# Graph-network kernel: the one-hot compares of the edge counting in four pieces of 8 slots instead of one of 32

## The reference, cut to what matters

```python
edge_index = jnp.stack([src, dst])
x = _layernorm(x + L0(x, src, dst, ...))          # attention over incoming edges
x = _layernorm(x + L1(x, edge_index, 3))          # three times: mean of the neighbours
x = _layernorm(x + L2(x, edge_index, edge_attr))  # edge network, maximum over edges
x = _layernorm(x + L3(x, edge_index))             # three times: normalised sum of the neighbours

# of L1 and L3, three times each:
summed = jax.ops.segment_sum(x[src], dst, num_segments=N)

# L0, the attention:
aij = (feat[dst] - feat[src]) @ (w2_W.T @ a_vec) + ...
m = jax.ops.segment_max(aij, dst); aexp = jnp.exp(aij - m[dst])
alpha = aexp / segment_sum(aexp, dst)[dst]
res = segment_sum(alpha[:, None] * (feat[src] @ w2_W.T + w2_b), dst)
```

## Time and profile before

| | us |
|---|---|
| median of 3 runs | 15430.6 (15423.8 to 15435.31) |
| span of the profiled execution | 14066.3 |
| of which POOL gathers in this stage, first start to last start | 495.7 to 5414.8 |
| POOL busy over the whole span | 8729.6 (62%) |
| PE busy | 9466.4 (67%) |
| DVE busy | 8214.5 (58%) |
| ACT busy | 6584.2 (47%) |

### The profile page before, as it was taken

The page is one execution under the profiler, slowest core; times in us unless marked ns, Lnnn a source line. Parts: engine busy times, 40 slices in busy tenths (PEclk is TensorE's granted clock), DMA queues, the critical chain, the costliest instruction groups (busy, mean ns, idle before and its releaser), DMA issues. The chain is left out here.

```text
span 14066.3 us, 164878 instructions
## 1 busy us (share of the span) xinstructions
PE 9466.4 (67%) x47732; PEld 6096.5 (43%) x47732; DVE 8214.5 (58%) x5617; ACT 6584.2 (47%) x6430; POOL 8729.6 (62%) x7438
## 2 busy tenths in 40 slices
PE   2355555555555552999998477767767674999998
PEld 2244444444444442555554233333333332555555
DVE  2366666666666666787877233333333333778877
ACT  1244444444444443888886122222222221888887
POOL 5777777777777776232324777777777776142323
PEclk7555555555555555999999666666666665999999
DMA  5233333333333332999998233333333332999998
GB/s 88 48 89 86 89 86 89 86 89 86 89 87 88 87 88 70 311 296 312 294 312 243 49 65 65 65 65 65 65 65 65 65 64 44 312 301 305 295 312 259
DMA packets 3238421, 1981.98 MB, mean 141 GB/s; under 512 B 1212287, under 2 KB 3140913, under 8 KB 3238257
## 3 DMA queue, kind: packets, MB, share of 16 engines
q1 hardware_dynamic: 2785457, 1664.63, 41.5%
q0 software_dynamic: 239424, 185.44, 7.5%
q10 hardware_dynamic: 213504, 131.51, 3.3%
HBM read 1602.28 MB, written 381.54 MB: 141 GB/s over the span
## 5 line engine op out<-in xcount | busy, mean ns | idle before, releaser
L624 POOL DMA_INDIRECT attend_and_count_rows<-table,attend_and_count_ring x3136 | 3917.4, 1249 | 1029.6 <-issue 1002.7
L1230 POOL DMA_INDIRECT judge_edges_rows<-table,judge_edges_ring x3128 | 2951.6, 944 | 1013.5 <-issue 988.6
L1133 POOL DMA_INDIRECT base<-slot_sums,last_slot x588 | 1273.2, 2165 | 2914.7 <-DMA slot_sums<-propagate_mean_out 1364.4
L659 PE MATMUL attend_and_count_counts<-attend_and_count_hot_hi,attend_and_count_hot_lo 128*128 128x98 bf16 x15680 | 1377.0, 264 | 2377.5 <-ACT attend_and_count_stage L769 1501.9
L1340 DVE TENSOR_TENSOR_SCAN judge_edges_feat<-judge_edges_keep,judge_edges_feat,judge_edges_p_feat 32x512 f32<-32x512 bf16 x782 | 960.1, 1265 | 2495.6 <-PE judge_edges_p_feat L1284 2474.3
L659 PEld LDWEIGHTS attend_and_count_counts<-attend_and_count_hot_hi,attend_and_count_hot_lo 128*128 128x128 bf16 x15680 | 1154.9, 130 | 2598.6 <-ACT attend_and_count_stage L769 1626.6
L1039 PE MATMUL propagate_mean_p_dense<-propagate_mean_part,propagate_mean_split 128*96 128x512 bf16 x9114 | 1994.3, 380 | 199.3 <-ACT propagate_mean_part L966 174.8
L1039 PE MATMUL propagate_norm_p_dense<-propagate_norm_part,propagate_norm_split 128*96 128x512 bf16 x9114 | 1992.8, 380 | 188.7 <-ACT propagate_norm_part L966 158.6
L966 ACT CAST propagate_norm_part<-propagate_norm_raw 128x7168 bf16<-128x7168 uint8 x282 | 1720.0, 6162 | 337.8 <-DVE propagate_norm_slot_sum L1088 296.1
L966 ACT CAST propagate_mean_part<-propagate_mean_raw 128x7168 bf16<-128x7168 uint8 x282 | 1720.0, 6162 | 336.7 <-DVE propagate_mean_slot_sum L1088 295.3
L687 DVE TENSOR_TENSOR attend_and_count_hot_hi<-ramp_hi,attend_and_count_key_hi 128x3136 bf16<-128x3136 bf16 x490 | 878.0, 1792 | 1359.8 <-ACT attend_and_count_key_lo L737 1349.0
(11 more groups left out here) (236 smaller groups left out, 10196.0 us busy)
## 6 DMA issues: line engine op xcount, KB each, us to landing
propagate_mean_raw<-matrix SPq DMA_DIRECT2D x651, 896.0 KB, 6.5
propagate_norm_raw<-matrix SPq DMA_DIRECT2D x651, 896.0 KB, 6.5
matrix<-attend_and_count_stage SPq DMA_DIRECT2D x245, 784.0 KB, 3.9
scan<-attend_and_count_out SPq DMA_DIRECT2D x784, 68.0 KB
inject<-attend_and_count_zeros SPq DMA_DIRECT2D x196, 256.0 KB, 2.0
attend_and_count_rows<-table,attend_and_count_ring POOLq DMA_INDIRECT x3136
judge_edges_rows<-table,judge_edges_ring POOLq DMA_INDIRECT x3128
judge_edges_rows<-inject SPq DMA_DIRECT2D x782, 64.0 KB
```

What stands on the lines that cost most here:

```text
L624: nc.gpsimd.indirect_dma_start(out=rows[:, u, g, j, :], out_offset=None, in_=D.table0[:, :], in_offset=rows_of(ring[:, u, g, j:j + 1])).th ...
L659: last = nc.tensor.matmul(counts[:, r % 2, k // 4, NH * (k % 4):NH * (k % 4) + NH], hot_lo[:, u, slot, :], hot_hi[:, u, slot, :], start=Tr ...
L1133: nc.gpsimd.indirect_dma_start(out=sums[:, h, :], out_offset=None, in_=D.slot_sums[0:blocks * BLOCK, :], in_offset=rows_of(S.last_slot[:, ...
L1230: nc.gpsimd.indirect_dma_start(out=rows[:, u, half, j, 0:FEAT], out_offset=None, in_=D.table2[:, :], in_offset=rows_of(ring[:, u, half, j: ...
```

## The change

Each sub's two compares become eight: for each quarter of 8 slots first `hot_hi`, then `hot_lo`, each with its own increment of `hot`, which now goes up by 8 for each sub. PE waits for a quarter's two compares before that quarter's matmuls. ACT's wait is rescaled to the new count. Elements compared, values, matmuls and casts are the same.

```diff
             def count(i, m):
...
-                pe.wait_ge(hot, s * 2 + 2)
                 for r in range(QUARTERS):
+                    pe.wait_ge(hot, s * (2 * QUARTERS) + 2 * (r + 1))
                     pe.wait_ge(staged[r % 2], s * 2 + r // 2)
...
                 dve.wait_ge(counted[u], n * QUARTERS)
-                for hots, ramp, two, width in ((hot_hi, S.ramp_hi, key2_hi, NH), (hot_lo, S.ramp_lo, key2_lo, P)):
-                    nc.vector.tensor_tensor(
-                        hots[:, u].rearrange("p v (h t) -> p v h t", t=2),
-                        ramp[:].rearrange("p (h t) -> p h t", t=2).unsqueeze(1).to_broadcast([P, SUB, width // 2, 2]),
-                        two[:, u].unsqueeze(2).to_broadcast([P, SUB, width // 2, 2]), ALU.is_equal).then_inc(hot, 1)
+                for r in range(QUARTERS):
+                    some = slice(r * SLOTS_Q, (r + 1) * SLOTS_Q)
+                    for hots, ramp, two, width in ((hot_hi, S.ramp_hi, key2_hi, NH), (hot_lo, S.ramp_lo, key2_lo, P)):
+                        nc.vector.tensor_tensor(
+                            hots[:, u, some].rearrange("p v (h t) -> p v h t", t=2),
+                            ramp[:].rearrange("p (h t) -> p h t", t=2).unsqueeze(1).to_broadcast([P, SLOTS_Q, width // 2, 2]),
+                            two[:, u, some].unsqueeze(2).to_broadcast([P, SLOTS_Q, width // 2, 2]), ALU.is_equal).then_inc(hot, 1)
...
-                act.wait_ge(hot, s * 2)
+                act.wait_ge(hot, s * (2 * QUARTERS))
```

## The result

The changed kernel took **16041.84 us** (4 runs, 16027.89 to 16053.94), the kernel before, on the same chip, 15427.2. The ratio is **1.0402 [1.0387, 1.0416]**: 4% slower, where 2.5% faster was forecast.

The account below looks back on a forecast made before the run. POOL's gather issues, held by DVE's compares, were taken to bound the changed stage. Shorter pieces would save 490 x 0.80 = 392 us: 15430.6 - 392, about 15040 us, range 14860 to 15240 (0.90).

Parts of the forecast that it names:

- The 1364.3 us between span and median are taken as unchanged: Whole kernel: the difference between the trace's span, 14066.3 us, and the timed median, 15430.6, stays as it is.
- POOL stays the bound: Changed stage: POOL still sets the pace of a 23.1 us step, ACT's standing for gathers shrinking from 8.7 to about 6.7.
- slower: Rival, POOL's issues: each waits for the whole compare chain's end, 820 us more, 16250 us; chance 0.05.
- the signs named for being wrong: Changed kernel's profile: pieces starting late behind an issue, issues above 2 us common, or POOL standing for ACT's `ring`.
- The pieces: DVE's compares: `hot_hi` pieces of 0.56 us, `hot_lo` of 0.68, a chain of 4.40 us where the pair took 3.99.
- POOL's waits: Gather issues (L624): 0.80 us less holding per pair, 392 us in all; mean falls from 1249 to about 1124 ns.
- DVE's added time is hidden: DVE in the changed stage: 200 us more work, covered by 1360 us of idle time ahead of `hot_hi`.
- ACT's idle ahead of `pack`: ACT's standing for gathered rows in the changed stage: falls by 300 to 400 us and stays above 1200.
- PE's waits cost nothing: PE's counting: three more waits and register instructions a sub, ahead of matmuls that stood idle 2377 us, cost nothing.
- the larger: Rival: issues at their best phase and L714's stretch gone, 564 us gained, 14870 us; chance 0.13 (below 14960).
- the smaller gain: Rival: dear pieces or the worst phase, 200 to 274 us gained, 15160 to 15230 us; chance 0.07.
- No change: Rival: compares are delayed 0.82 us at each of three grants, or the stretch has another cause; 15430 us; chance 0.05.

Follow-up runs that it names:

- e13: The changed kernel, unchanged, run again on a chip of the shorter kind: 13665.24 us against 14075.79 for the kernel before, ratio 0.9707.
- e8: The changed kernel with one gather a step instead of 16 in attend-and-count: 14188.48 us, longer kind.
- e16: The changed kernel with 8 of the 16 gathers of a step: 14574.52 us, longer kind.
- e1: The kernel before, unchanged, run again with its own span and profile: 15406.08 us, ratio 0.9995, longer kind.
- e6: Against the kernel before, each compare in two pieces of 16 slots instead of the change's four of 8: 15628.7 us, ratio 1.006, longer kind.
- e9: The changed kernel with a DVE memset of 192 elements between the second and third pair of pieces: 16239.3 us, ratio 1.0481, longer kind.
- e3: The changed kernel, but only the last piece of each kind raises `hot`, PE and ACT waiting as before: 16281.47 us, ratio 1.0468, longer kind.
- e10: The changed kernel with two small memsets on POOL ahead of each attend-and-count gather: 16342.48 us, ratio 1.0538, longer kind.
- e12: The changed kernel with 16 plain copies a step by SP in place of POOL's attend-and-count gathers: 13147.3 us, shorter kind.
- e15: The changed kernel with 16 plain copies a step by SP in place of POOL's attend-and-count gathers, on the longer kind: 14520.54 us.
- e4: The kernel before, compares whole, but PE waits before each of the four quarters: 15493.72 us, ratio 0.9974, longer kind.
- e11: The kernel before with 16 plain copies a step by SP in place of POOL's attend-and-count gathers: 13104.54 us, shorter kind.
- e7: The kernel before with one gather a step instead of 16 in attend-and-count: 14089.13 us, longer kind.

## Why the prediction was wrong, point by point

**Where it failed.** The first step that failed is "The 1364.3 us between span and median are taken as unchanged." A span 9% below the timed runs wasn't something around the span here: every later execution has its time as its span (15403.9 and 15406.08; 16042.5 and 16041.84). The 1364 us were the other kind of chip. Of the 1338 us between the two spans 1179 lie in the edge stage (5134 against 3955 us from first to last gather), and the stage that is changed differed by only 24 us before (4943 against 4919), because ACT's slack hid its late starts. So the trace showed ACT 8.7 us of slack a step where the timed runs had 5.3 (1030 us by 196), and none of its late starts. The second step rests on it: "POOL stays the bound", with ACT's slack at 6.7 us a step. On the longer kind the pieces left ACT 0.7 us a step (134 by 196), and POOL stood 946 us for ACT's `ring`. The chance of 0.05 for slower, and a range that ended at 15240, rest on that slack.

**What took its place.** Of the signs named for being wrong the last did come: POOL began to stand for `ring`. In the changed kernel on the longer kind ACT starts its casts long after PE's quarter and ACT's own work are done. Timelines of PE and ACT there:

```profile
3050.84 1.51 PE L659 MATMUL attend_and_count_counts<-attend_and_count_hot_hi,attend_and_count_hot_lo 128*128 128x98 bf16 x16
3052.66 0.54 PE L659 MATMUL attend_and_count_counts<-attend_and_count_hot_hi,attend_and_count_hot_lo 128*128 128x98 bf16 x8 [0.30 <-issue]
```

```profile
3051.79 0.81 ACT L771 CAST attend_and_count_stage<-attend_and_count_counts 128x784 uint8<-128x784 f32 x1 [1.50 <-PE attend_and_count_counts L659]
3054.16 0.81 ACT L771 CAST attend_and_count_stage<-attend_and_count_counts 128x784 uint8<-128x784 f32 x1 [1.55 <-PE attend_and_count_counts L659]
3055.63 0.81 ACT L771 CAST attend_and_count_stage<-attend_and_count_counts 128x784 uint8<-128x784 f32 x1 [0.66 <-PE attend_and_count_counts L659]
```

PE's second quarter is done at 3052.35 and ACT is free at 3052.60; its cast starts at 3054.16. The third quarter is done at 3053.20, ACT is free at 3054.97, the cast starts at 3055.63. Of the 1960 casts 806 start over 0.3 us after both PE's quarter and ACT's own work had ended, 2100 us in all; on the shorter kind none does. 170 are late by 0.6 to 0.7 us, 104 by 1.2 to 1.4, 76 by 2.0 to 2.2: peaks 0.70 us apart. But 115 are late by over 5 us, the worst by 21.5, and these bring 968 of the 2100.

It isn't ACT that is slow to start. What comes late is the increment of the semaphore for which it waits, and that is one of PE's. In this stage the trace has 2145 increments that PE's work makes, and 1051 of them are recorded over 0.2 us away from the end of any PE work that makes them; of the 2735 recorded ones of ACT's work and the 3357 of DVE's none is. On the shorter kind none of PE's 2315 is (e13); on the longer it is none of 2243 with one gather a step (e8), 611 of 2199 with eight (e16), and 951 of 1231 in the edge stage. 785 of the 806 late casts have the increment of `counted` within 0.1 us of their start, and in 774 PE had begun the next quarter before. PE's own quarters, which wait for ACT and DVE, begin on time: 17 of 1958 are over 0.3 us late, 9 us in all. And in the edge stage DVE, which waits there for PE, starts late as ACT does. Its scan on the shorter kind and on the longer (the changed kernel both times):

```profile
L1342 DVE TENSOR_TENSOR_SCAN judge_edges_feat<-judge_edges_keep,judge_edges_feat,judge_edges_p_feat 32x512 f32<-32x512 bf16 x782 | 960.0, 1265 | 2500.2 <-PE judge_edges_p_feat L1286 2494.6
```

```profile
L1342 DVE TENSOR_TENSOR_SCAN judge_edges_feat<-judge_edges_keep,judge_edges_feat,judge_edges_p_feat 32x512 f32<-32x512 bf16 x782 | 960.1, 1265 | 3525.7 <-remote 2842.2 <-issue 364.2 <-PE judge_edges_p_feat L1286 319.2
```

The traces of the longer kind lack many increments, of every engine (2735 of ACT's 3859 in this stage are there), so this holds for the recorded ones; and the ends of matmuls are modelled by the profile, so it doesn't tell whether PE's work ends late or its increment travels late. From there the way to the loss is argued, not tested step by step: casts that wait make ACT list late, POOL stands for the list, the gathers end late, and the slack that POOL's gain should have been paid from is gone.

**What stays open** is how shorter compares make more late increments of the same gathers. The traces show which casts are hit. Of those that fall due while POOL is in a gather of under 1.2 us, one that isn't held, 92 of 549 are over 0.3 us late in the kernel before (e1; 116 us of 722 in all) and 392 of 577 in the changed one (1340 us of 2100); for the longer gathers it is 284 of 1028 (283 us) and 267 of 657 (366 us), for POOL in no gather 124 of 383 (322 us) and 147 of 726 (394 us). So most of the added harm sits beside gathers that run free, though hardly more casts fall due there. The order of e1, e6, the changed kernel and e9 (holding 992, 781, 727 and 508 us; stage 4943, 5091, 5555 and 5702 us, on different chips) would fit, but not e3 beside the changed kernel, and e10, whose gathers were spaced, kept its late starts. I call it a place, not a cause. Nor is it shown what differs between the two kinds of chip. The mean granted TensorE clock does not tell them apart by itself: it is 0.58 in this stage in the trace and 0.54 in e1, but 0.59 in both e12 and e15, where no increment comes late.

**What held, on the kind of chip that the trace came from:**
- *The pieces.* 0.56 and 0.68 us forecast, 0.559 and 0.682 measured; chain 4.40 and 4.40. Right, on either kind.
- *POOL's waits.* L624's mean at 1124 ns forecast, 1120 measured; 404 us saved (3917.4 - 3513.6) against 392; the last gather at 5023 forecast, 5010.7 measured. Right. Two issues of 3136 lasted over 3.5 us.
- *DVE's added time is hidden.* Idle ahead of `hot_hi` went from 1360 to 797 us. Right; where POOL no longer sets the pace the pieces do cost, 43 us (e12 less e11) to 99 us (e8 less e7).
- *ACT's idle ahead of `pack`.* Forecast down by 300 to 400 and above 1200: from 1709 to 1284, 425 down. Right but for 25 us.
- *PE's waits cost nothing.* Right, by e4.

**The rivals.** On the shorter kind neither the larger nor the smaller gain was needed: 411 us lies between the forecast's own 274 and 470. "Slower" had its mechanism seen right and its weight wrong: on the longer kind 84 issues, against 490 chains, wait for the end of a whole chain or nearly so, 311 us in all, but e9 takes these holds away and gains nothing, so they are not what makes it slower. Its ground, that a boundary between short pieces is missed in general, is false: on the shorter kind 2 issues last so long, and on the longer most get through too. "No change" supposed that compares are delayed by issues; the pieces keep 0.56 and 0.68 us in both kinds.

The inference in the Trainium skill, "SBUF — State Buffer", section "Who interferes with whom", that making descriptors isn't held up by such an instruction, doesn't fit these runs for gathers that read their offsets from SBUF: cutting the instruction shorter gave back 404 us of POOL's issues on the shorter kind. Whether the read of the offsets or the making of descriptors is what waits is not shown.

## What to carry to other kernels

Before any slack is read from a profile, set its span beside the timed runs: a gap of 9% was here another condition of the machine, not time outside the kernel, and the slack in the profile was not the slack of the runs. Where POOL's indirect gathers set the pace, as here, judge a change on both kinds of chip: what POOL gained was worth its time only where ACT, which lists for POOL, kept slack. When an engine starts late behind a done releaser, look where the semaphore's increment is recorded before blaming the engine that waits. The hold itself is real and was cut: an issue that meets one of these compares waits for its end, and shorter ones gave back 404 us.

## What the runs showed of the hardware

- Two kinds of chip for the same program: 14055 to 14076 us on three, 15416 to 15533 us on four here; all runs on one chip stayed in one kind. Where POOL gathers nothing the kinds agree to 0.01% of a stage (4016.2 and 4015.8 us); where it gathers 3128 times, one takes 3955 and the other 5187 us, while the gathers themselves last the same (943 to 946 ns).
- On the longer kind, while POOL gathers, about half of PE's recorded semaphore increments are recorded over 0.2 us away from the end of the work that makes them (1051 of 2145 in the changed kernel's stage); the casts that wait for them start late by amounts that peak 0.70 us apart and reach 21.5 us. None of ACT's 2735 or DVE's 3357 is.
- 0.81 to 0.83 us from the end of the compare that holds an issue to the end of the issue, in the rows shown, for pieces of 0.56 us as for compares of 2.28 us.
- An issue that asks within 0.3 us of a chain's start, or 1.2 to 1.3 us after it, can miss all the boundaries between back-to-back pieces that are left (5.24 us at most): of 3136 issues 84 last over 3.5 us in the changed kernel on the longer kind, all but two of them asked there, and 2 on the shorter. One memset between pieces, by which the chain grows from 4.40 to 4.55 us, ends that (no issue over 3.1 us in e9).
